# Unpacking four-bit weights: whole codes on VectorE, sign and magnitude on GpSimd

## What is computed

```python
NVFP4_LUT = jnp.array([0.0, 0.5, 1.0, 1.5, 2.0, 3.0, 4.0, 6.0, 0.0, -0.5, -1.0, -1.5, -2.0, -3.0, -4.0, -6.0])
low = W_packed & 15
high = W_packed >> 4 & 15
idx = jnp.stack([low, high], axis=-1).reshape(N, -1)
vals = NVFP4_LUT[idx]
vals = vals.reshape(N, K // block, block) * scales[:, :, None]
...
inter = gelu(xt @ Wg.T) * (xt @ Wu.T)
out = inter @ Wd.T
```

## Time and profile before

| what | value |
|---|---|
| median of 3 runs | 1719.08 us (1718.13 to 1724.01) |
| the profiled execution's own time | 1715.61 us |
| its span | 1713.8 us |
| TensorE matmul busy (PE) | 1622.4 us, 95% |
| VectorE (DVE) busy | 1148.4 us, 67% |
| ScalarE (ACT) busy | 950.1 us, 55% |
| GpSimd (POOL) busy | 544.9 us, 32% |

### The profile page before, as it was taken

How to read it: one execution, slowest core, us unless ns; L and a number is a source line. 1 busy time by engine, 2 the same in 40 slices (tenths; PEclk the granted TensorE clock), 3 DMA queues, 4 the chain that set the end, 5 groups by cost and what they waited for, 6 DMA issues and landing times. The chain is left out here.

```text
span 1713.8 us, 33133 instructions
## 1 busy us (share of the span) xinstructions
PE 1622.4 (95%) x13534; PEld 1065.5 (62%) x13534; DVE 1148.4 (67%) x1670; ACT 950.1 (55%) x1889; POOL 544.9 (32%) x454
## 2 busy tenths in 40 slices
PE   6799999999999989999997999999999998999998
PEld 5454444554445568888885644455544456888887
DVE  6448988688876366554746589877888645755454
ACT  2225677766787624444432357877678763444443
POOL 5212667787778413333330010000000000333333
PEclk9789999999999999999999999999999999999999
DMA  5114316115102060000004242340510104200000
GB/s 139 51 33 57 54 47 111 48 40 93 47 25 80 34 277 24 1 1 1 1 0 148 75 57 44 38 63 2 70 32 2 39 2 201 96 13 1 13 13 12
DMA packets 50491, 89.34 MB, mean 52 GB/s; under 512 B 20921, under 2 KB 35001, under 8 KB 48073
## 3 DMA queue, kind: packets, MB, share of 16 engines
q1 hardware_dynamic: 45560, 70.99, 17.6%
q0 software_dynamic: 4256, 15.78, 2.9%
q10 hardware_dynamic: 528, 0.52, 0.1%
HBM read 58.17 MB, written 28.84 MB: 51 GB/s over the span
## 5 line engine op out<-in xcount | busy, mean ns | idle before, releaser
L1177 DVE TENSOR_REDUCE chunk_max<-ring 128x2 f32<-128x1024 f32 (+3 forms) x640 | 669.4, 1063 | 163.0 <-PE ring L909 105.4
L1072 ACT ACTIVATE probs<-ps_s 128x512 f32<-128x512 f32 (+3 forms) x1280 | 619.4, 535 | 263.2 <-PE ps_s L940 144.4
L1497 POOL TENSOR_TENSOR inter_lo<-inter,inter_hi 128x512 fp32r<-128x512 f32 x128 | 165.8, 1295 | 838.6 <-ACT inter_hi L1447 838.6
L935 PE MATMUL ps_s<-xnt 64*128 64x512 f32 (+3 forms) x640 | 240.6, 427 | 5.8 <-ACT probs L1072 5.6
L909 PE MATMUL ring<-xnt 63*128 63x512 f32 (+3 forms) x640 | 210.8, 450 | 25.5 <-DVE chunk_max L1177 7.2
L935 PE MATMUL ps_s<-region_rounded 64*128 64x512 f32 (+3 forms) x640 | 228.4, 440 | 4.5 <-ACT probs L1072 4.2
L909 PE MATMUL ring<-region_rounded 63*128 63x512 f32 (+3 forms) x640 | 226.1, 428 | 5.0 <-DVE chunk_max L1177 4.0
L935 PEld LDWEIGHTS ps_s<-xnt 64*128 64x128 f32 x640 | 107.4, 187 | 123.9 <-ACT probs L1072 99.8
L1428 ACT ACTIVATE gelu_a<-ps_g 128x512 f32<-128x512 f32 x128 | 76.6, 599 | 194.1 <-PE ps_u L87 194.0
L954 PE MATMUL ps_o<-probs,region_plain 128*32 128x256 f32 (+1 forms) x2304 | 177.2, 379 | 1.3 <-ACT probs L1072 1.3
L954 PE MATMUL ps_o<-probs,unit_plain 128*32 128x256 f32 (+2 forms) x2176 | 176.5, 396 | 1.8 <-ACT probs L1072 1.8
(11 more groups left out here) (209 smaller groups left out, 2852.6 us busy)
## 6 DMA issues: line engine op xcount, KB each, us to landing
w_mlp<-w_scr SPq DMA_DIRECT2D x32, 768.0 KB, 14.7
w_scr<-region_rounded POOLq DMA_DIRECT2D x16, 768.0 KB, 3.8
region_rounded<-q_scr SPq DMA_DIRECT2D x24, 256.0 KB, 8.4
q_scr<-region_rounded SPq DMA_DIRECT2D x16, 192.0 KB, 2.4
xnt<-q_scr SPq DMA_DIRECT2D x12, 256.0 KB, 8.2
xnt<-w_scr SPq DMA_DIRECT2D x4, 768.0 KB, 5.5
q_scr<-region_rounded SPq DMA_DIRECT2D x8, 384.0 KB, 3.6
k_scr<-region_rounded SPq DMA_DIRECT2D x8, 384.0 KB, 3.6
```

Of the source, the lines that this page charges most:

```text
L935: op = pe.matmul(out[:, 0:TW - w0], kt[g][shifted[h % 2], (h // 2) % NKP, kb * P:(kb + 1) * P], qt[g][shifted[h % 2], h // 2, t * TW + w0: ...
L1072: act.activation(pr[n % NPR][:, h, w0:TW], src[:, 0:TW - w0], ACT.Exp, scale=SCALE).then_inc(s_e, 1)
L1177: dve.tensor_reduce(mp[rank[y[1:3]] % 2][:, qb, 2 * p:2 * p + 2, c], ring[n % 2][:, :, 0:w], AX.X, ALU.max).then_inc(s_rd, 1)
L1497: pool.tensor_tensor(il[n % NI][:, :], ti[n % 2][:, :], ih[n % NI][:, :].bitcast(F32), ALU.subtract).then_inc(s_il, 1)
```

## The change

VectorE takes the whole four-bit code of each nibble with one operation, where it took magnitude and sign with one each. The two integer buffers `mg` and `sg` become one, `vg`. GpSimd copies the code v to float, compares it with 7.5 (8.0 where it is smaller, 0.0 where not), adds that, which gives the magnitude plus 8 in either case, and makes +0.5 or -0.5 out of the comparison's result. The two operations with a maximum have their constants moved by the 8, and read the float buffer in place of the integers. Each operation up to that point waits for the one before it. `CH` goes from 8 to 10.

```diff
--- before.py
+++ after.py
@@ -118,7 +118,7 @@
         self.io, self.per = io, per
         NI = 3 * P
         self.pk = [carve.take((NI,), I32) for _ in range(2)]
-        self.mg, self.sg = (carve.take((NI, 2), I32) for _ in range(2))
+        self.vg = carve.take((NI, 2), I32)
         self.r1, self.r2, self.mf, self.sf = (carve.take((NI * 2,)) for _ in range(4))
         self.wv, self.wt = (carve.take((2 * NI,)) for _ in range(2))
         self.st = [carve.take((2, WCH), F32R) for _ in range(2)]
@@ -143,8 +143,7 @@
         dve.wait_ge(self.s_ld[b], 48 * (j // 2 + 1))
         dve.wait_ge(self.s_wv, j)
         for k in range(2):
-            dve.tensor_scalar(self.mg[:, :, k], self.pk[b][:, :], 4 * k, 7, ALU.logical_shift_right, ALU.bitwise_and)
-            op = dve.tensor_scalar(self.sg[:, :, k], self.pk[b][:, :], 4 * k + 3, 1, ALU.logical_shift_right, ALU.bitwise_and)
+            op = dve.tensor_scalar(self.vg[:, :, k], self.pk[b][:, :], 4 * k, 15, ALU.logical_shift_right, ALU.bitwise_and)
         op.then_inc(self.s_x, 1)
 
     def transpose(self, pe, j, part, out):
@@ -162,7 +161,7 @@
 
         flat = lambda x: x[:, :, :].rearrange("p n k -> p (n k)")
         r1, r2, mf, sf = self.r1[:, :], self.r2[:, :], self.mf[:, :], self.sf[:, :]
-        CH = 8
+        CH = 10
         for j in range(NF):
             n, b = j, j % 2
             done = [0]
@@ -175,13 +174,14 @@
             pool.wait_ge(self.s_x, n + 1)
             if n + 2 < NF:
                 self.load(pool, n + 2)
-            pool.tensor_copy(mf, flat(self.mg)).then_inc(self.s_c, 1)
+            step(pool.tensor_copy(mf, flat(self.vg)))
+            step(pool.tensor_scalar(sf, mf, 7.5, 8.0, ALU.is_lt, ALU.mult))
+            step(pool.tensor_tensor(mf, mf, sf, ALU.add))
+            pool.tensor_scalar(sf, sf, 0.125, -0.5, ALU.mult, ALU.add).then_inc(self.s_c, 1)
             done[0] += 1
-            pool.tensor_scalar(r1, flat(self.mg), 4.0, -16.0, ALU.max, ALU.add).then_inc(self.s_c, 1)
+            pool.tensor_scalar(r1, mf, 12.0, -48.0, ALU.max, ALU.add).then_inc(self.s_c, 1)
             done[0] += 1
-            pool.tensor_scalar(r2, flat(self.mg), 6.0, 2.0, ALU.max, ALU.mult).then_inc(self.s_c, 1)
-            done[0] += 1
-            step(pool.tensor_scalar(sf, flat(self.sg), -1.0, 0.5, ALU.mult, ALU.add))
+            step(pool.tensor_scalar(r2, mf, 14.0, 2.0, ALU.max, ALU.mult))
 
             step(pool.tensor_tensor(r1, r1, r2, ALU.add))
             step(pool.tensor_tensor(mf, mf, r1, ALU.add))
```

## The result

| | before | changed |
|---|---|---|
| median, 4 runs each | 1718.74 us | 1747.5 us (1742.83 to 1750.11) |
| ratio, 95% interval | | 1.0152 [1.013, 1.0175] |
| the profiled execution's own time | 1715.61 us | 1750.11 us |

A forecast was written before the change was run, and what follows sets the result against it. TensorE's stream was taken to bound the stretch of packed weights. Stalls of 22.0, less 4.8 of VectorE's gain, plus 1.5 of clock gave +18.7 us, 1737.8 us against the median; the range was 1717 to 1750.

The forecast's parts named there:

- The price of the comparison: GpSimd's added `is_lt` with `mult` before `wv`: taken as 2.78 us, like a maximum, since no row showed it.
- a: Time added to GpSimd's loop per chunk by the comparison and the addition: 4.77 us, or 2.82 with a cheap comparison.
- The stalls: TensorE waiting for GpSimd's `wv` before transposes in chunks 2, 3, 6, 7, 9, 10, 12 and 13: 22.0 us.
- The gain of VectorE: Fewer unpacking operations in the first attention: 8.8 us on offer, from waits 4.5, clock 3.3 and two other chunks 1.0.
- the collisions: VectorE's unpacking slowed where it meets GpSimd's work; three TensorE waits for a maximum, 4.5 us, should go.
- The cap of 4.8 us: Limit on VectorE's gain, as chunks earlier on TensorE still wait for GpSimd: 4.8 of the 8.8 us count.
- The clock term: Half clock on TensorE after stalls, costing only behind those of chunks 3 and 13: 1.5 us at even odds.
- 32.6 us of idle: GpSimd's idle time in the first and last two chunks, taken to hide the extra work there at no cost.
- The cheap comparison: Rival one: GpSimd's comparison takes 0.83 us, stalls of 8.2 us, total +1 us or 1720; chance 0.18.
- Cheap maxima: Rival two: GpSimd's two maxima fall to 0.83 us on float input, 1710 or about 1711 us; chance 0.07.
- rival four: Stalls absorbed as ScalarE and VectorE catch up: 4 us off the forecast; shares the forecast's 0.63 chance.
- rival three: GpSimd's comparison dearer than a maximum, 3.8 us: stalls sum to 31.5, total +31 or 1750 us; chance 0.12.

The follow-up runs named there:

- e2: Kernel before with the same comparison and an addition added on GpSimd ahead of `wv`, VectorE's old unpacking kept: 1748.23 us, ratio 1.0157.
- e1: Changed kernel without GpSimd's added comparison and addition, so its chain has the old length (values wrong): 1709.28 us, ratio 0.9938.
- e11: Changed kernel without the comparison and addition, and with GpSimd's cast waiting for VectorE's next unpacking (values wrong): 1706.67 us, ratio 0.9932 against the kernel before.
- e9: Kernel before with one wait added: GpSimd's cast of a chunk waits until VectorE has unpacked the next chunk: 1706.01 us, ratio 0.9928.
- e7: Changed kernel with small matmuls on TensorE filling the stalls before the transposes of eight chunks: 1747.88 us, ratio 1.0164 against the kernel before.
- e6: Changed kernel without the comparison and addition in chunk 14 alone (that chunk's values wrong): 1743.01 us, ratio 1.0139 against the kernel before.
- e5: Changed kernel with the comparison replaced by a cheap multiply-add on the same buffers (values wrong): 1726.43 us, ratio 1.0045 against the kernel before.

## Why the prediction was right in direction and short in size

- *The price of the comparison* held to the digit: 2.78 us, and a = 4.77. The maxima kept theirs. The Trainium skill (GPSIMD Engine Reference, section 4.1 Engine selection) calls one-input elementwise operations roughly line-rate. The trace agrees only for the pair of product and sum (0.62 us for 512 columns, 0.83 for 768) and for the copies and casts (0.82 to 0.84 for 768), while the maximum and the comparison, and the product alone, take 1.5 to 1.9 for 512 columns.
- *The stalls* are where rows 4 put them. Eight waits for GpSimd sum to 20.1 us against the 22.0 worked out, the longest, 4.27 before chunk 6, against 4.21 there. They don't match in every chunk: chunk 8 waited 1.28 us and chunk 9 not at all, where the reverse was forecast. Before chunk 7 TensorE waited 1.44 us where 4.60 were worked out, since behind chunk 6's stall it worked at the half clock (0.50 over 365 to 372 us) and came late to chunk 7's transposes by itself. e2 has the same waits with the old unpacking, so they come from the chain alone.
- *The gain of VectorE* was sized right by itself (8.8 forecast, about 10 in e1). That e11 is no faster than e9 shows that the two operations fewer add nothing that can be measured once the collisions are gone. The part of the 8.8 us that was to come from the clock is not borne out: e1's mean clock is the 0.98 of before. The cap of 4.8 us was still too generous: e2 and the change are alike.
- *The clock term* of 1.5 us was too small. I let the half clock cost only where the next chunk had time of its own. But it also slows the transposes and so GpSimd's loop, which waits for them: a chunk's six take 1.51 or 1.52 us in chunks 6, 12 and 13 and 0.85 in 3 and 7, and idle before the cast is 2.25 us or 2.26 there against 1.64. e7 prices it at 3.6 us, from one profile of each kernel.
- *The step that failed* is "I cost at nothing the extra GpSimd work in the first and last two chunks, hidden in their 32.6 us of idle". The idle time covers GpSimd's own lateness. It does not cover VectorE, whose layer norm of the last tile fell under the longer chain of chunk 14. That is 6.8 us in the profiled execution, shown by e6's profile; the medians of the change and e6 lie 4.5 us apart, which is within their scatter.
- In sum, for chunks 1 to 13: 22.0 of stalls and 3.6 of clock make 25.6, 24.3 were measured, so about 1.3 us of VectorE's gain would survive there. The 22.0 are the forecast's; with the 20.1 us of waits in the trace nothing of the gain is left. e2, with the old unpacking, takes 336.0 us for the same chunks, 1.1 more than the change, so what survives is a microsecond or nothing. With 6.8 for chunk 14 the loss is 31 us, against a difference of medians of 28.8.
- *The rivals.* The cheap comparison was forecast at +1; e5, which has its price, lost 8. The interval with the layer norm is 3.4 of that. The clock may be a part again (0.97 from 168 to 600 us, before 0.98), which no run separates. Cheap maxima and a dearer comparison did not occur. Nor were the stalls absorbed, as rival four had it: 20.1 us of waits made the stretch 24.3 us longer. The collisions as a reason for a faster kernel were real, up to 12 us in e9, but only without the longer chain.
- *Luck.* The measured 1747.5 us lies nearer to rival three's 1750 than to the forecast's 1737.8. The range reached that far for a comparison dearer than a maximum, which is not what happened; the layer norm and the clock filled the space.

What stays open: whether any of the 3.9 us behind chunk 14 belongs to the change, whether e5's missing microseconds are all clock, and why the wait of 1.81 us at 407.82 shrinks in e9 and not in e11.

## What to carry to other kernels

When a step is taken from one engine and given to another, read the receiving engine's idle time at each iteration and against the instruction it ends in. A mean idle time of 6 us per chunk hid two chunks with 0.2 and 0.6 us of slack. Work hidden in one engine's idle time can still slow another engine, as GpSimd's did VectorE's layer norm here, so look at what runs under the longer stretch. Before cutting operations, look for the few that take several times their usual time: here one wait, which lets the short operations of VectorE pass before GpSimd's long ones, brought all that halving them did.

## What the runs showed of the hardware that was not expected

- On GpSimd at 128x512 in float, `tensor_scalar` with a product alone took 1.50 us, with product and sum 0.62 us. By these rows adding the sum makes the product cheaper.
- A VectorE operation on 4 columns took up to 1.67 us when a GpSimd operation was running, the integer `tensor_scalar` and the two-input form alike, where it takes 0.16 to 0.17 otherwise. Two that began at 580.50 and 582.41 us, 0.01 us before the next GpSimd operation, kept their 0.17 and 0.16.
- Waits of TensorE of 1.2 to 1.8 us were followed by the 1.2 GHz level in some places and not in others. In the kernel before, the clock was 0.59 over 388 to 392 us behind a wait of 1.48 us, 0.66 over 465 to 470 behind 1.25 and 0.57 over 408 to 412 behind 1.81, but 1.00 over 280 to 284 behind 1.77. In e1 it was 0.50 over 204 to 208 us behind waits of 0.82 and 0.43 us.
- In e9, whose waits at these four places are at most 1.06 us, the clock over 168 to 600 us was 1.00 where it was 0.98.
